# An opening in another order, eight PSUM banks in one store, and a lead for each row and layer in a four-row transformer kernel

## What is computed

```python
x = x + tanh(g_xattn[0]) * L0_xattn(layernorm(x), ctx, adj, mask)      # 16 heads of 8, additive adj, mask
x = x + tanh(g_ffn[0])   * L0_ffn(layernorm(x))                        # 8 tiles, argmax picks one
x = x + tanh(g_xattn[1]) * L1_xattn(layernorm(x), ctx)                 # 16 heads, q/k RMS norm, rope, causal
x = x + tanh(g_ffn[1])   * L1_ffn(layernorm(x))                        # 8 LoRA experts, top 2
x = x + tanh(g_xattn[2]) * L2_xattn(layernorm(x), ctx, mask)           # 4 heads of 32, rope
x = x + tanh(g_ffn[2])   * L2_ffn(layernorm(x))                        # 8 experts 128 -> 512, argmax
x = x + tanh(g_xattn[3]) * L3_xattn(layernorm(x), ctx)                 # 16 heads
x = x + tanh(g_ffn[3])   * L3_ffn(layernorm(x))                        # the outputs of tokens 0..511 only
```

## Time and profile before

| | us |
|---|---|
| median of 3 runs | 1077.09 |
| lowest and highest of the 3 | 1071.6, 1079.28 |
| the profiled execution | 1068.41 |
| its span, first to last instruction | 1066.7 |

### The profile page before, as it was taken

One profiled execution on the slowest core, in us unless ns is written; L12 is line 12 of the kernel. 1 busy time (PEld: TensorE's weight loads), 2 busy tenths in 40 slices (PEclk: granted clock), 3 DMA queues, 4 the chain that ended last, 5 costly groups with the idle time before them and its releaser, 6 DMA issues.

```text
span 1066.7 us, 19274 instructions
## 1 busy us (share of the span) xinstructions
PE 880.5 (83%) x7316; PEld 573.0 (54%) x7316; DVE 787.8 (74%) x1849; ACT 493.7 (46%) x753; POOL 302.4 (28%) x324
## 2 busy tenths in 40 slices
PE   1778787788899998887898877787888999998686
PEld 1533346454566676663465323564456667776443
DVE  3899998778666945449778999878779574554783
ACT  2655453345534532217874656234554343322475
POOL 3600246443443211100323023655335330110000
PEclk9999777698989999988999989677998999988899
DMA  9100000000000000000110000000000000000000
GB/s 322 33 2 2 2 1 1 1 2 2 2 1 2 2 1 6 6 1 2 42 32 21 2 2 1 1 1 2 3 3 1 1 2 1 1 1 1 2 7 17
DMA packets 11741, 14.26 MB, mean 13 GB/s; under 512 B 1604, under 2 KB 10716, under 8 KB 11396
## 3 DMA queue, kind: packets, MB, share of 16 engines
q1 hardware_dynamic: 11552, 12.88, 3.7%
q10 hardware_dynamic: 100, 0.14, 0.1%
HBM read 11.55 MB, written 1.05 MB: 12 GB/s over the span
## 4 chain that ended last, share of the span: by engine, by line
PE 43%; DVE 40%; ACT 7%; issue 6%; SPq 1%; DMA 1%; POOL 1%; DVEq 0%; ACTq 0%
PE banks L986 36%; DVE nm_row L1440 13%; DVE probs L1459 5%; PE pv L986 4%; ACT probs L943 2%; DVE qf_row L1470 2%; DVE wide L1529 2%; DVE st_row L1283 2%; PE banks L682 2%; DVE xn_row L1395 1%; DVE mv_row L1285 1%; DMA xn_row<-in_ctx 1%; ACT wide L965 1%; ACT qT_row L860 1%; ACT kT_row L860 1%
## 5 line engine op out<-in xcount | busy, mean ns | idle before, releaser
L1440 DVE TENSOR_REDUCE nm_row<-banks 128x4 f32<-128x1024 f32 (+1 forms) x192 | 210.3, 1128 | 39.2 <-PE banks L986 38.6
L776 POOL TENSOR_TENSOR rstd_row<-rstd_row,neghalf 128x2 f32<-128x2 f32 x66 | 47.6, 721 | 365.8 <-DVE rstd_row L1390 277.8
L943 ACT ACTIVATE probs<-banks 128x1024 f32<-128x1024 f32 (+1 forms) x144 | 128.2, 933 | 36.5 <-PE banks L986 35.9
L986 PE MATMUL banks<-wide,c 128*128 128x256 f32 x512 | 127.9, 406 | 0.0
L986 PE MATMUL banks<-qT_row,kT_row 50*128 50x256 bf16 (+2 forms) x896 | 89.9, 298 | 29.6 <-DVE nm_row L1440 15.6
L986 PE MATMUL pv<-probs,vpad 128*32 128x256 f32 (+1 forms) x1536 | 105.7, 395 | 9.8 <-ACT probs L938 6.6
L986 PE MATMUL banks<-kT_row,qT_row 48*128 48x256 bf16 (+2 forms) x896 | 92.3, 294 | 25.7 <-DVE nm_row L1440 15.7
L986 PEld LDWEIGHTS banks<-wide,c 128*128 128x128 f32 x512 | 101.0, 202 | 18.3 <-issue 0.9
L938 ACT ACTIVATE probs<-probs 128x1024 f32<-128x1024 f32 x64 | 67.5, 1056 | 50.0 <-DVE probs L1459 48.1
L986 PE MATMUL banks<-c,wide 128*128 128x128 f32 x512 | 85.4, 336 | 3.7 <-POOL wide L834 3.7
L986 PEld LDWEIGHTS banks<-c,wide 128*128 128x128 f32 x512 | 79.6, 245 | 8.1 <-issue 6.4
(11 more groups left out here) (220 smaller groups left out, 1585.5 us busy)
## 6 DMA issues: line engine op xcount, KB each, us to landing
c<-in_c SPq DMA_DIRECT2D x1, 2500.0 KB
wide<-in_mask SPq DMA_DIRECT2D x8, 256.0 KB, 2.9
qT_row<-mT_row SPq DMA_DIRECT2D x96, 4.0 KB
c<-in_c SPq DMA_DIRECT2D x1, 1194.5 KB
xn_row<-in_ctx SPq DMA_DIRECT2D x8, 128.0 KB, 3.5
x_row<-in_x SPq DMA_DIRECT2D x8, 128.0 KB, 2.4
late<-in_late SPq DMA_DIRECT2D x2, 512.0 KB, 15.4
out<-x_row SPq DMA_DIRECT2D x8, 128.0 KB, 2.0
```

Source lines behind the costliest of these rows:

```text
L776: return pool.tensor_tensor(t, t, neghalf[:, 0:n], ALU.pow)
L943: act.activation(dst[:, :, 0:w], src[:, :, 0:w], ACT.Exp, scale=1.0 if l == 2 else HD ** -0.5).then_inc(sem["probs"], 1)
L986: return pe.matmul(dst, lhsT, rhs, start=start, stop=stop, **kw)
L1440: V.tensor_reduce(nm[b][:, t, :, 2 * jp:2 * jp + 2], ps[:, :, :, 0:kn], AX.X, ALU.max, negate=True).then_inc(sem["max"], 1)
```

## The change

Three things change; the arithmetic of every step stays as it is.

1. The opening. On SP's queue the order was: `c0`, context, mask, tokens of row 2, context of row 3, the strips, the four packs and `late`, mask and tokens of row 3, context of rows 1 and 0, and so on. Now `c0` comes without its last 512 columns (`adj`), which follow behind the tokens of row 0 with a semaphore of their own; contexts and tokens come ahead of masks; the packs come behind all four masks; `late` is a step of its own behind layer 0. The strips are issued by ACT. `picks` and `small` land in the `late` buffers instead of the `probs` buffers, so `attend` needs neither `split` nor `fold` of layer 0 any more.
2. PSUM. `BANKS` is 8; `pv` is no tensor of its own, but `weigh` claims one bank of the common store (`pv_ps`) until `divide` has read it.
3. The rule of turns. `LEAD` has a number for each row and layer instead of one for each row, and eleven entries of `COST` are altered and one is new. This gives other lists on all engines.

```diff
-STACKS, WIDES, PROBS, BANKS = 3, 2, 4, 7
+STACKS, WIDES, PROBS, BANKS = 3, 2, 4, 8
...
-    out = [("mask", 0, row), ("fetch", 0, row)] + k[0] + k[2] + k[3] + k[4] + [("bias", 0, row)]
+    out = [("fetch", 0, row), ("mask", 0, row)] + ([("consts", 0, row)] if row == ROWS - 1 else []) + k[0] + k[2] + k[3] + k[4] + [("bias", 0, row)]
     for l in range(4):
         wide = l != 2
+        out += [("late", 0, row)] if (l, row) == (1, 0) else []
...
-LEAD = [280.3, 290.2, 324.8, 314.7, 4.7, -4.1, 22.7, 13.6]
+LEAD = [[264.3, 260.0, 262.6, 273.2], [309.7, 298.4, 297.5, 298.2], [326.4, 329.7, 320.3, 322.1], [302.7, 296.9, 283.1, 302.2], [158.0, -1.2, 156.1, 2.7], [-13.0, 3.9, -25.3, -15.8], [56.9, 16.3, 22.9, 13.5], [32.2, 10.2, -2.2, -6.2]]
...
-        ("kv", 2): [("PE", .5), ("DVE", 2.5)],
+        ("kv", 2): [("PE", .5), ("DVE", 2.87)],
...
-    if l >= 1 or kind in ("attend", "o_flip", "route", "choose", "spread", "outer"):
+    if l >= 1 or kind in ("route", "choose", "spread", "outer"):
         if eng != "SP":
             out.append((("fold", 0, 0), eng))
-    if kind == "attend" and eng in ("ACT", "DVE"):
+    if kind == "late":
+        out.append((("split", 0, ROWS - 1), "DVE"))
+    if kind == "consts":
+        out += [(("mask", 0, r), "SP") for r in range(ROWS - 1)]
+    if kind == "fold" and eng in ("ACT", "DVE"):
         out.append((("split", 0, ROWS - 1), eng))
...
+    if kind == "weigh" and s[3] == 0:
+        out.append(("pv_ps", "one", ("sums", l, row)))
...
-            return (-left[s, eng] - LEAD[s[2]], s[2])
+            return (-left[s, eng] - LEAD[s[2]][s[1] % 4], s[2])
...
-        picks = probs[0][0:16, :, :].rearrange("p r n -> p (r n)"), probs[1][0:16, :, :].rearrange("p r n -> p (r n)")
-        small, rest = (t[0:3 * E, :, :].rearrange("p r n -> p (r n)") for t in (probs[2], probs[1]))
+        picks = late[0][0:16, :], late[1][0:16, 0:2 * P]
+        small, rest = late[1][0:3 * E, 2 * P:FF3], late[0][0:3 * E, :]
...
-        pv = ctx.enter_context(nc.psum_tensor("pv", [P, 512], F32))
...
-                sp.dma_start(pack["c0"][:, :], dram["c0"]).then_inc(early_in, 16)
+                adj = WHERE["adj"][1]
+                sp.dma_start(pack["c0"][:, 0:adj], dram["c0"][:, 0:adj]).then_inc(early_in, 16)
...
+                    if kind == "late":
+                        sp.wait_ge(setup_dve, 7)
+                        for i in range(2):
+                            sp.dma_start(late[i][:, :], dram["late"][:, i * FF3:(i + 1) * FF3]).then_inc(late_in, 16)
                     if kind == "consts":
-                        sp.wait_ge(setup_zero, 1)
-                        for j in range(2):
-                            for c in range(LANES):
-                                at_row, head = COLS * c + j * (HD + 1), LANES * j + c
-                                sp.dma_start(spreads[at_row:at_row + HD + 1, :], dram["spreads"][head * (HD + 1):(head + 1) * (HD + 1), 0:P]).then_inc(const_in, 16)
                         for n in LATE_PACKS:
                             sp.dma_start(pack[n][:, :], dram[n]).then_inc(const_in, 16)
-                        for i in range(2):
-                            sp.dma_start(late[i][:, :], dram["late"][:, i * FF3:(i + 1) * FF3]).then_inc(late_in, 16)
...
+                        if row == 0:
+                            sp.dma_start(pack["c0"][:, adj:WIDTH["c0"]], dram["c0"][:, adj:WIDTH["c0"]]).then_inc(adj_in, 16)
...
+                        pool.wait_ge(adj_in, 16)
...
+                act.wait_ge(setup_zero, 1)
+                for j in range(2):
+                    for c in range(LANES):
+                        at_row, head = COLS * c + j * (HD + 1), LANES * j + c
+                        act.dma_start(spreads[at_row:at_row + HD + 1, :], dram["spreads"][head * (HD + 1):(head + 1) * (HD + 1), 0:P]).then_inc(strips_in, 16)
...
-                            ended = turn_before(l, row)
-                            if ended:
-                                pe.wait_ge(sem[ended[0]], plan.value[ended])
+                            claim(pe, "pv_ps", s)
+                        pv = bank("pv_ps", ("weigh", l, row, 0))
...
+                        pe.wait_ge(strips_in, 16 * 2 * LANES)
```

33 lines of the change are left out of this document (18 added, 15 removed).

## The result

The changed kernel takes **1089.67 us** in the median of 6 runs (1082.27 to 1095.21), the kernel before 1077.09 us in 6 runs beside it (1071.6 to 1081.12). The ratio is **1.0126** (95% interval 1.0077 to 1.0175): slower by 1.3%, less than 2% but clear of its interval, where I had forecast 1060 us and 1.6% faster. The profiled execution took 1088.58 us, its span 1086.9 us, its mean granted clock 0.887; before it was 1068.41, 1066.7 and 0.902. Four executions in a slower state of the machine (1155.78 us of `e11_nudge`, 1251.06 of `e13_last_leads`, 1085.64 and 1085.45 of the kernel before) are in no ratio of this text.

What follows compares the result with a forecast made beforehand. No single engine was taken to bound the kernel: DVE or PE by stretches, neither in the first 48 us. Gains of 8 + 2 + 7 = 17 us took 1068.4 to 1051.4, plus 8.7 for the runs' median: 1060 us, range 1038 to 1082.

Steps and rivals of the forecast that it cites:

- Part 1: Opening, ahead of layer 0's first reduce: contexts ahead of the packs win 8.0 us for good; bounds 5.5 to 12.
- The rival of the opening that fails: Packs land after DVE is ready for the fold, or POOL's biases hold the first layer norm: 1068 to 1072; chance 0.05.
- That the shift of row 2 would queue behind the packs: Opening, SP's DMA queue: row 2's small shift transfers would wait behind the packs; no separate size given.
- Part 2: PSUM store: an eighth bank, shared with pv, wins 2 us; bounds 2 lost and 6 won.
- Part 3: New order: 7 us won where rows 4 to 7 follow the first four, bounds 0 and 14; 0 elsewhere.
- I count 0 for it, with 10 us to either side: Rest of the lists, new succession of rows: same work on each engine, so no gain or loss, 10 us either way.
- the change of rows: First four rows to second four, 528 to 576 us: filling half of DVE's 14.2 us idle wins 7 us.
- The clock: Whole kernel, PE: more time at the low clock level, 28 us lost, 1088 us; chance of above 1077: 0.12.
- My signs: Profile after: contexts land below 6 us, first reduce at 36 to 42, row 6's first reduce some 15 us earlier, seven low-clock slices.
- my three signs of failure: First reduce moves under 8 us; windows behind 672 us lose the first half's gain; mean clock leaves 0.902 by over 0.02.

Runs made afterwards that it cites:

- e11_nudge: Kernel before with only row 6's lead altered, 20.7 instead of 22.7: ratio 1.0308, 1108.97 us.
- e13_last_leads: Changed kernel with the old leads for rows 0 to 3 and the new ones for rows 4 to 7: ratio 1.0219, 1099.61 us.
- the opening alone: Kernel before with only the new opening; seven banks, old leads and old costs except SP's loads: ratio 0.9950, 1069.25 us.
- banks alone: Kernel before with eight banks and pv claimed from the common store, lists made anew by the plan: ratio 1.0130, 1091.07 us.
- leads alone: Kernel before with the new table of leads and the new costs, its opening and banks kept: ratio 1.0553, 1137.21 us.

## Why the prediction was wrong

**Part 1, 8.0 us, was right in its mechanism and near in size.** The first reduce came 9.1 us earlier (I had 9.8, of which 1.8 are the fold that only moves), the packs were issued at 27.93 us for my 29, landed by 43.63 for my 45, and the fold stood at 59.37 for my 58. The gain for good was 0.68% with the old lists behind it (0.9932), 7.3 us of 1077, and 0.50% with the plan's own (0.9950), 5.4 us, just below my lower bound of 5.5; with eight banks beside it, 0.29% (0.9971). The intervals of the three overlap. The rival of the opening that fails is out. That the shift of row 2 would queue behind the packs could not show: it is issued at 58.04 us, 14 us after they landed.

**Part 2, 2 us, was right within what can be measured**: with the lists kept the eighth bank gives 0.9991, and PE's waits for reduces are 37.0 us in that kernel for 39.2, which agrees with the reason that I gave (a bank more only lets PE wait later) but is one profile against one. But I had priced a bank and not what the plan does with it. That costs 1.4% (1.0130 against 0.9991).

**Part 3 is the step that failed**, in both of its terms. "If all idle time were filled, 14.2 us would be won; since PE must make the scores for those reduces in the full stretch, I take half, 7 us": tried alone, it lost 20. I had named PE's part and priced it as half a gain that is missed. It was a loss: scores and reduces of rows 6 and 7 went in front of row 0's last steps, and the handover that the next rows wait for came 18 us later. And I had read DVE's idle time as room, though the stretch behind it is not shortened by work that is taken out of it, since row 4's start takes 23 us all the same. In the 48 us ahead of the last `deep_out` DVE's idle time is 14.8 us before and 10.8 in the changed kernel, so some was filled, for nothing.

One reading under this term was false as well. I wrote that row 6 is not begun from 528 to 576 us, its statistics at 536.75. By the list of DVE those are row 1's, ahead of its `deep`; the wait of 3.90 us is row 1's `o_flip`. Row 6's keys stood at 514.71 and its statistics here:
```profile
525.49 0.61 DVE L1283 BATCH_NORM_STATS2 st_row<-x_row 128x6 f32<-128x128 f32 x2
```
So row 6 was already under way before that stretch, and there was less to draw ahead than I believed.

"I count 0 for it, with 10 us to either side": this was the larger error. I argued that the work on each engine is the same and PE's 186 us of idle time are many small waits. The runs show that for these lists 0 is not the middle. In the changed kernel itself 18.6 us of row 0 are gone in layer 0, the place that I had put at nothing. Eight kernels have the old leads or a neighbour of them and lists made anew by the plan for some small difference, or with a few steps moved (0.995, 1.005, 1.010, 1.010, 1.013, 1.019, 1.019, 1.031): seven of the eight are slower. Kernels with the new table or a part of it in the plan have 1.013 to 1.055. The old lists behave like a picked draw: nearly everything else loses, up to 5.5%, and a term for "another order" has its middle at a loss of 1 to 2% and not at 0. Of the 15 kernels with changed lists that came out slower, 12 lose over 1.2%, 13 us, which is beyond the 10 us that I had allowed.

**The plan's own time had much of this.** The plan ends with a number of its own, `plan.time`: when the last step ends by the times of `COST`. It comes out of the kernel's text without the chip, and my prediction did not use it. For the kernel before it is 1017.1 us. With one of the eight old leads moved by 0.5, 1, 2 or 5 us, up or down, all 64 neighbours end later, by 2.7 to 44.0 us. Row 6's lead less 2 us gives 28.6 us (measured 34.5 by the medians), row 2's plus 2 gives 11.7 (measured 19.6). Of the 64 neighbours of the new table that are 2 us away 57 end later, 7 at the same time and none earlier. Both tables stand at a low point of this number, so the new one looks picked too, and a change of any input leaves such a point. Over the 19 changed kernels the differences of `plan.time` to the kernel before and those of the measured medians go together (correlation 0.92; half of them agree within 6.5 us, the worst is 19.5 off). It does not order kernels that are close: it has the new leads 7.9 us better than the old ones (1022.6 against 1030.5), where the runs have them 0.8% worse, and it has the opening alone 5.5 us worse than the kernel before, where the runs have it better.

**The sum by rows of experiments**, along one path: opening 0.9950; with the plan's lists for eight banks 1.0102; new costs 1.0050; new leads 1.0126. That is -5, +16, -6 and +8 us. The path is not the only one. On seven banks the same table loses 5.5%.

**Inside the new leads** the trace shows where row 0 falls behind: with the new leads of the first four rows alone it leaves layer 3 at 568.1 us, with the old ones at 551.3, and the whole change has 577.8. But these four are not the whole loss, since the new leads in the last four rows alone lose more (1.0219 against 1.0155). That leads which let two rows run side by side give the time to the row that needed it least is argued from the traces; no run shows it. Only the change of rows was tried by itself.

**The clock** was my rival on the other side, and it gave the right number, 1088, by luck. I let it decide from 61 us more at the low level. The engine is at either of two levels, 1.2 and 2.4 GHz, so a mean of 0.902 is 209 us at the lower one and 0.887 is 246: 37 us more. PE is busy 891.3 us for the same 7316 matmuls, where it was 880.5. So 10.8 of the 20.2 us between the two profiles are matmuls that took longer, and the rest is waiting. Against the kernel before, each 100 us more at the low level go with 28 to 32 us more of busy PE in the rows of this table (26 to 68 in the other kernels):

| kernel | ratio | clock | PE busy, us | at the low level, us |
|---|---|---|---|---|
| before | 1 | 0.902 | 880.5 | 209 |
| old lists, eight banks | 0.999 | 0.902 | 878.7 | 209 |
| after | 1.013 | 0.887 | 891.3 | 246 |
| banks alone | 1.013 | 0.865 | 907.3 | 295 |
| row 6's lead -2 | 1.031 | 0.860 | 912.9 | 312 |
| leads alone | 1.055 | 0.851 | 916.9 | 339 |

That agrees in direction with the sentence of the Trainium skill that I had quoted (TensorE: Matmul & The Clock Gate, Part 1: The HAM clock gate), by which the throttled state is the default and activity releases it.

But the profile of the kernel before has a higher clock than most of its runs, and the runs tell more. In the sets of the experiments its clock is on record for 69 executions, 0.876 to 0.906, with the same lists. The 13 with 0.900 or more took 1070.2 us in the mean, the 9 with 0.880 or less 1079.7: so much goes with the clock at fixed lists. In 21 of them it lies from 0.883 to 0.888, as in all six of the changed kernel, and they took 1077.1 us in the mean (1072.29 to 1083.85), the changed kernel 1089.7. So at the same mean clock the changed kernel is still slower by 12.6 us, as much as its median lies above the other's. The mean clock does not explain that. (The chip of the changed kernel's set is not on record; from set to set the median of the kernel before moves from 1072.98 to 1077.09.) What remains open is whether it matters at which steps the clock is low.

**My signs.** The slowest context of the opening landed in 5.3 us (I had said below 6), no DMA in the chain behind 12 us but the shift of row 2 at 60.23, PE's waits for reduces at 31.8 (below 39), seven slices of low clock, the mean within 0.02: all came true. No `weigh` waited for a bank that a reduce held. DVE's idle time ahead of the last `deep_out` fell, but not to half. Row 6's first reduce comes 31.0 us behind the last `mix` of row 2, whose `store` follows, and came 41.8 before: 10.7 us earlier, where I had said 15. The first reduce moved by more than 8 us. None of my three signs of failure came as I had worded it. The nearest is that the windows behind 672 us would lose what the first half wins; the loss came long ahead of them, in layer 0, and from row 5's layer 0 on (27.2 us late) to the end (20.1) some is won back.
